# Attention layer with its LayerNorm, router and next-batch input taken from between the batches into the per-head units

## What is computed

```
x = L0_attn_x                                  # (4, 1024, 512) float32
x = x + layernorm(attention(layernorm(x)))     # 4 groups x 4 heads, causal, D = 128
x = x + layernorm(ffn(layernorm(x)))           # top 4 of 32 experts, and a shared expert
# attention: q = rope(x w_aq), k = rope(x w_ak), v = x w_av, softmax(q k + mask) v, times w_ao
# ffn begins with h = rmsnorm(x) * norm_w and logits = h @ router_w.T, of which the top 4 are kept
```

## Time and profile before

| | |
|---|---|
| median of 3 runs | 3898.41 us (3894.68 to 3900.13) |
| profiled execution: its own time | 3902.94 us |
| its span | 3901.0 us |
| PE busy | 3450.9 us, 88% |
| DVE busy | 2377.4 us, 61% |
| ACT busy | 1544.9 us, 40% |
| POOL busy | 1449.2 us, 37% |

### The profile page before, as it was taken

One profiled execution on the slowest core, in us unless ns is written; L12 is line 12 of the kernel. 1 busy time (PEld: TensorE's weight loads), 2 busy tenths in 40 slices (PEclk: granted clock), 3 DMA queues, 4 the chain that ended last, 5 costly groups with the idle time before them and its releaser, 6 DMA issues. The chain is left out here.

```text
span 3901.0 us, 71161 instructions
## 1 busy us (share of the span) xinstructions
PE 3450.9 (88%) x20374; PEld 2950.1 (76%) x20375; DVE 2377.4 (61%) x5034; ACT 1544.9 (40%) x3460; POOL 1449.2 (37%) x1569
## 2 busy tenths in 40 slices
PE   6999996899999699999959999994898999989987
PEld 5888886788888578888858888883687777777766
DVE  5666666666666666666666666667664444444448
ACT  2443443334434243543524344342122444444443
POOL 2333331233333133333303333332422555545548
PEclk9999997899999699999969999995999999999999
DMA  1100002000000200000020000015333676767768
GB/s 54 29 15 15 29 15 100 4 26 17 15 26 17 98 12 18 23 18 18 23 93 15 15 29 15 15 44 203 126 112 95 155 196 159 175 165 171 166 148 277
DMA packets 183202, 287.34 MB, mean 74 GB/s; under 512 B 16544, under 2 KB 69024, under 8 KB 182848
## 3 DMA queue, kind: packets, MB, share of 16 engines
q1 hardware_dynamic: 150432, 204.57, 16.1%
q0 software_dynamic: 32416, 78.43, 10.2%
HBM read 201.93 MB, written 81.02 MB: 73 GB/s over the span
## 5 line engine op out<-in xcount | busy, mean ns | idle before, releaser
L424 DVE TENSOR_TENSOR ptl<-TP,pth 128x512 fp32r<-128x512 f32 (+1 forms) x640 | 407.9, 637 | 281.2 <-ACT pth L560 270.2
L282 POOL TENSOR_SCALAR oTh<-onorm 128x256 fp32r<-128x256 f32 x256 | 104.3, 407 | 1000.3 <-DVE onorm L430 1000.3
L560 ACT CAST pth<-TP 128x512 fp32r<-128x512 f32 (+1 forms) x640 | 349.5, 546 | 300.9 <-PE TP L696 297.1
L613 PE MATMUL O<-pth,vh 128*128 128x256 f32 (+1 forms) x1280 | 399.9, 312 | 22.7 <-DVE ptl L424 22.7
L274 POOL TENSOR_TENSOR work<-work,cst 128x320 f32<-128x320 f32 x128 | 132.9, 1038 | 735.2 <-ACT work L544 735.2
L412 DVE TENSOR_REDUCE negmax<-S 128x1 f32<-128x384 f32 (+7 forms) x512 | 382.3, 749 | 15.9 <-PE S L681 11.1
L613 PE MATMUL S<-wph,xTh 128*128 128x512 f32 (+1 forms) x1024 | 354.6, 346 | 7.0 <-DVE xTl L369 6.7
L615 PE MATMUL O<-pth,vl 128*128 128x256 f32 (+1 forms) x1280 | 359.4, 281 | 0.0
L614 PE MATMUL O<-ptl,vh 128*128 128x256 f32 (+1 forms) x1280 | 358.4, 280 | 0.0
L614 PE MATMUL S<-wpl,xTh 128*128 128x512 f32 (+1 forms) x1024 | 347.2, 339 | 0.0
L615 PE MATMUL S<-wph,xTl 128*128 128x512 f32 (+1 forms) x1024 | 345.7, 338 | 0.0
(11 more groups left out here) (279 smaller groups left out, 9323.1 us busy)
## 6 DMA issues: line engine op xcount, KB each, us to landing
raww<-in_L_ffn_w_dram SPq DMA_DIRECT2D x33, 1024.0 KB, 7.3
prob<-in_L_attn_x_dram SPq DMA_DIRECT2D x9, 2048.0 KB, 9.4
stage<-in_L_attn_w_aq_dram SPq DMA_DIRECT2D x68, 256.0 KB, 2.8
raww<-in_L_ffn_w_dram SPq DMA_DIRECT2D x33, 512.0 KB, 8.2
stage<-in_L_attn_w_ao_dram SPq DMA_DIRECT2D x64, 256.0 KB, 2.6
a<-acc_d SPq DMA_DIRECT2D x64, 256.0 KB, 4.1
acc_d<-x SPq DMA_DIRECT2D x1, 8448.0 KB, 31.5
x_d<-racc SPq DMA_DIRECT2D x4, 2048.0 KB, 14.2
```

The source lines that it names most:

```text
L282: nc.gpsimd.tensor_scalar(slot(oTh, u), onorm[:], 1.0, 1.0, ALU.mult, ALU.mult).then_inc(o_hi, 1)
L424: nc.vector.tensor_tensor(ptl[:, n % 2, 0:w], TP[:, n % 2, 0:w], pth[:, n % 2, 0:w].bitcast(F32), ALU.subtract).then_inc(tp_lo, 1)
L560: nc.scalar.copy(pth[:, n % 2, 0:w], TP[:, n % 2, 0:w]).then_inc(tp_hi, 1)
L613: mm(out, ah, bh, start=first, stop=False)
```

## The change

The work between batches is cut into tiles of 128 tokens and put beside the units. Iteration (b, g) finishes tiles 2g and 2g+1 of batch b-1 and makes tiles 2g and 2g+1 of the x of batch b+1 (modulo 4, so the first batch "finishes" zeros and the last makes an x that is not used). `racc` of a batch is stored to a DRAM tensor `r_d` at its end, and the tiles' transposed x goes to the DRAM tensors `xt_d`, from which `xTh` and `xTl` are reloaded whole, 4 MB, by POOL at unit 12 of the last iteration of a batch. The tiles live in four slots, `slotA` to `slotD`, of the array `work`, and the second half of `S[:, 1]`, called `side`, takes their transposes and logits. Standard deviations come from POOL's `pow` in place of ACT's square root; the logits are plain float32 matmuls, one per 128 rows of h in place of three. The last batch is finished behind the loop, tile after tile.

The tables give the unit at which each step of the two tiles stands: `XN` statistics of x, `XH` its normalisation, `XT_AT` its transpose and split; `RS`, `RN` the same statistics and normalisation of r; `RA` adding x and the statistics of the sum; `RH` its normalisation and product with norm_w; `HT_AT` the transpose of h; `LG_AT` logits and top four.

```diff
+XN, XH = {0: 0, 8: 1}, {1: 0, 9: 1}
+XT_AT = {2: 0, 10: 1}
+RS = {2: 0, 9: 1}
+RA = {3: 0, 11: 1}
+RN = {3: 0, 10: 1}
+RH = {4: 0, 12: 1}
+HT_AT = {6: 0, 14: 1}
+LG_AT = {8: 0, 15: 1}
+EXTRA = {2: 1, 6: 2, 8: 3, 10: 4, 14: 5, 15: 6}
...
+            def scale_shift(done, sem, value, mean, var, sc, ready):
+
+                nc.gpsimd.tensor_scalar(sc[:, 2:3], var, LN_EPS, 1.0, ALU.add, ALU.mult).then_inc(sem, 1)
+                wait_apart(pool, sem, done + value + 1)
+                nc.gpsimd.tensor_tensor(sc[:, 0:1], sc[:, 2:3], half[:], ALU.pow).then_inc(sem, 1)
+                wait_apart(pool, sem, done + value + 2)
+                nc.gpsimd.tensor_scalar(sc[:, 1:2], mean, sc[:, 0:1], -1.0, ALU.mult, ALU.mult).then_inc(ready, 1)
...
+                        if u == RELOAD and reload:
+                            wait_apart(pool, xt_out, it * 64 + 80)
+                            for n, part in enumerate((xTh, xTl)):
+                                nc.gpsimd.dma_start(part[:], xt_d[n]).then_inc(xt_in, 16)
+                        if u in XN:
+                            wait_apart(pool, stx_ready, it * 2 + XN[u] + 1)
+                            scale_shift(pl0, pl, XN[u] * 10, mvx[:, 0:1], mvx[:, 1:2], scx, scx_ready)
...
+                        if u in RA:
+                            wait_apart(pool, str_ready, it * 4 + RA[u] * 2 + 2)
+                            norm_scale(pl0, pl, RA[u] * 10 + 4, mvr[:, 0:1], mvr[:, 1:2], sch, mr, scr_ready)
                         if h == 0:
...
-                            nc.vector.tensor_tensor(racc[:, t], racc[:, t], bank("r", t), ALU.add).then_inc(o_free, 1)
-
-                            wait_apart(v, o_free, b * MB + g * MG + (OUTPUTS.index(("r", t)) + 1 + 2))
-                            nc.vector.bn_stats(stat[:, t], racc[:, t]).then_inc(dve, 1)
...
+                        if u in XT_AT:
+                            k = XT_AT[u]
+                            v.wait_ge(xp_hi, it * SIDE + (EXTRA[u] + 1))
+                            if k:
+                                v.wait_ge(xt_out, it * 64 + (32 + 16))
+                            nc.vector.tensor_tensor(slotC.bitcast(F32R), side, slotB, ALU.subtract).then_inc(xp_lo, 1)
...
+                        if u in RS:
+                            k = RS[u]
+                            v.wait_ge(rd_in, it * 32 + (16 * k + 16))
+                            step(nc.vector.bn_stats(st1[:], slotD), STEPS[("r", k)])
+                            nc.vector.bn_aggr(mvr[:], st1[:]).then_inc(str_ready, 1)
+                        if u in RA:
+                            k = RA[u]
+                            v.wait_ge(rn_done, it * 4 + (2 * k + 1))
+                            v.wait_ge(ra_in, it * 32 + (16 * k + 16))
+                            nc.vector.tensor_tensor(slotD, slotD, slotA, ALU.add).then_inc(x2_ready, 1)
+                            v.wait_ge(x2_ready, it * 2 + (k + 1))
+                            step(nc.vector.bn_stats(st1[:], slotD), STEPS[("a", k)])
+                            nc.vector.bn_aggr(mvr[:], st1[:]).then_inc(str_ready, 1)
...
+                        beside(u)
                         norm_out(u)
                     add_results(PROJECT_LAST)
-                k = k0
-                base2 = v.snap(base + G * GD)
...
+                            nc.scalar.activation(slotD, slotD, ACT.Identity, bias=scr[:, 1:2], scale=scr[:, 0:1]).then_inc(rn_done, 1)
...
+                        beside(u)
                         act.wait_ge(pv_done, it * NPAIR + PAIR_OF[(u, ib)] + 1 + 2)
...
+                        if a == 1 and u - 3 in EXTRA:
+                            if u - 3 in XT_AT:
+                                pe.wait_ge(xp_lo, it * 2 + (XT_AT[u - 3] + 1))
+                            else:
+                                pe.wait_ge(xp_hi, it * SIDE + (EXTRA[u - 3] + 1))
...
+                            for c in range(MC):
+                                ins = nc.tensor.transpose(side[:, c * P:(c + 1) * P], slotA[:, c * P:(c + 1) * P], ident)
+                            ins.then_inc(xp_done, 1)
+                        if u in LG_AT:
+                            pe.wait_ge(xp_hi, it * SIDE + EXTRA[u])
+                            for c in range(MC):
+                                ins = mm(side[:, 0:E], slotB[:, c * P:(c + 1) * P], rwT[:, c], start=c == 0, stop=c == MC - 1)
+                            ins.then_inc(xp_done, 1)
```

More of the change, by code:

```diff
@@ new lines, in _ @@
+            with sp.Fori(0, B - 1) as b:
+                with sp.Fori(0, G) as g:
+                    iteration(b, g)
+                sp.wait_ge(o_free, b * (G * MG) + (G * MG + 2))
+                sp.dma_start(r_d[b].rearrange("(t p) m -> p t m", p=P), racc[:]).then_inc(r_out, 16)
+            with sp.Fori(0, G) as g:
+                iteration(B - 1, g)
+            sp.wait_ge(tp_done, NT + B * G * TG)
+            sp.dma_start(xin, x[B - 1].rearrange("(t p) m -> p t m", p=P)).then_inc(x_in, 16)
@@ L291, in _ @@
                             split_proj(n, it * 10 + 10, it * 80 + 80)
+                    if reload:
+                        landed = pool.to_reg(b * 32 + 32)
+                        pool.wait_ge(xt_in, 32)
+                        pool.wait_ge(xt_in, landed)
+                        pool.sem_inc(xt_ready, 1)
+            with pool.Fori(0, B - 1) as b:
+                with pool.Fori(0, G - 1) as g:
+                    iteration(b, g, False)
+                iteration(b, G - 1, True)
+            with pool.Fori(0, G) as g:
+                iteration(B - 1, g, False)
+            count = 0
+            for k, i in SCALED:
+                t = FINAL[i]
+                pool.wait_ge(str_ready, Z4 + SCALED.index((k, i)) + 1)
+                if k == 0:
+                    scale_shift(ZP, pl, count, mv[:, t, 0:1], mv[:, t, 1:2], fsc[:, t], scr_ready)
+                    count += 2
+                else:
+                    norm_scale(ZP, pl, count, mvh[:, t, 0:1], mvh[:, t, 1:2], fsh[:, t], fmr[:, t], scr_ready)
+                    count += 6
         @block.vector
@@ L327, in link, with stats @@
                 return k + 1
[L329 to L334, removed]
+            def stats(src_of, base, k):
+                for t in range(NT):
+                    nc.vector.bn_stats(stat[:, t], src_of(t)).then_inc(dve, 1)
+                k += NT
                 wait_apart(v, dve, base + k)
@@ L356, in _, with iteration @@
                 center(t, xin[:, t], xin[:, t]).then_inc(xln_ready, 1)
[L358 to L372, removed]
-                    it = v.snap(b * G + g)
-                    gb = v.snap(base + k0 + g * GD)
-                    hi0 = v.snap(hib + NT + g * TG)
+            for t in range(NT):
+                v.wait_ge(tp_hi, t + 1)
+                c4 = xTl[:, :, t * P:(t + 1) * P]
+                nc.vector.tensor_tensor(c4, TP[:, t % 2].rearrange("p (c n) -> p c n", c=MC),
+                                        xTh[:, :, t * P:(t + 1) * P].bitcast(F32), ALU.subtract).then_inc(tp_lo, 1)
+            def iteration(b, g, copies):
+                if True:
+                    it = v.snap(b * G + g)
+                    gb = v.snap(it * GD + first)
+                    hi0 = v.snap(it * TG + NT)
+                    tile = v.snap((b + B - 1) % B * NT + g * 2)
+                    dl0 = it * 12
+                    v.wait_ge(h_out, it * 32 + 16)
                     def lo_tile(t):
@@ L478, in _ @@
[L478 to L498, removed]
@@ new lines, in _ @@
+            act.wait_ge(h_out, 16 + 32 * B * G)
+            act.wait_ge(xt_out, 16 + 64 * B * G)
+            for kind, i in NORMAL:
+                t = FINAL[i]
+                if kind == 0:
+                    act.wait_ge(scr_ready, Z4 + SCALED.index((0, i)) + 1)
+                    nc.scalar.activation(racc[:, t], racc[:, t], ACT.Identity, bias=fsc[:, t, 1:2], scale=fsc[:, t, 0:1]).then_inc(rn_done, 1)
+                elif kind == 1:
+                    act.wait_ge(scr_ready, Z4 + SCALED.index((1, i)) + 1)
+                    nc.scalar.activation(work[:, t], racc[:, t], ACT.Identity, bias=fsh[:, t, 1:2], scale=fsh[:, t, 0:1]).then_inc(rn_done, 1)
+                elif kind == 2:
+                    act.wait_ge(tp_done, ZT + i + 1)
+                    if i >= 2:
+                        act.wait_ge(xp_done, ZX + i - 1)
+                    nc.scalar.copy(stage[:, i % 2], TP[:, i % 2]).then_inc(xp_hi, 1)
+                else:
+                    act.wait_ge(xp_done, ZX + i + 1)
+                    if i >= 2:
+                        act.wait_ge(dl, ZD + LINKS[i - 2])
+                    nc.scalar.copy(lgt[:, i % 2], O[:, i % 2, 0:E]).then_inc(tp_hi, 1)
```

378 lines of the change are left out of this document (252 added, 126 removed).

## The result

The changed kernel takes 3836.7 us (median of 4, 3832.7 to 3845.6) against 3896.6 us of the kernel before beside it (median of 4): a ratio of 0.985, 95% interval 0.983 to 0.987, some 60 us faster. The forecast was 26 us faster, a median of 3872 us. Its direction and the wide range (3795 to 3945 us) hold; the gain is 2.3 times the forecast one, and the time lies outside the forecast's own 3848 to 3896 us.

The account below looks back on a forecast made before the run. PE was taken as nearly full inside iterations and idle between batches. From the profiled 3902.9 us: -228.7 + 12 - 4.3 - 6 + 200 = 3875.9, so a median of 3872 us; range 3795 to 3945 us.

Parts of the forecast that it names:

- What bounds the kernel, and what goes: PE nearly full inside iterations, idle between batches; three gaps go, 228.7 us, plus 4.3 at the start, 6 at the end.
- What is added: Tile work in each of 16 iterations: 12.5 us exposed per iteration, 200 us in all; bounds 8 and 17.5 us.
- Units 9 and 10: Second half of an iteration: statistics, transposes ACT waits for, a copy and an Identity, 1.6 us exposed.
- Units 14 and 15: End of an iteration: the added tile work there was put at 1.5 us exposed.
- The wait for the reload: Between batches: PE waits 4 us each time for xTh and xTl, 12 us in all; bounds 0 and 56 us.
- Unit 2 and unit 3: First half: statistics, sum and ACT's work ahead of onorm delay ptl, stalling PE 1.6 and 2.0 us.
- Unit 12: POOL splits unit 11 behind norm_scale, making ACT 2.8 us late; half covered, so 1.4 us an iteration.
- Rival (a): Inside iterations the chain has more room than single slacks say: 8 us an iteration, 3800 us; chance 0.18.
- Rival (b): POOL's small operations wait 0.4, not 0.1 us, delaying ACT at units 3 and 11: 4 us an iteration, 3936 us; chance 0.16.
- Rival (c): Between batches the reload is late, a second 18.8 us each time: 3928 us; chance 0.12.
- Rival (d): Float32 logits take several passes: 43 us more, 3915 us, or 3894 with unit 15's hidden; chance 0.07.
- Rival (e): Stalls of 2 us lower PE's clock inside iterations, one unit at half pace each: 78 us, 3950 us; chance 0.05.

Follow-up runs that it names:

- dup_r: Changed kernel with the statistics of the sum of results taken twice on DVE, in units 2 and 9; 3856.8 us, an iteration 1.1 us longer.
- behind_rh: Changed kernel with POOL's norm_scale behind the output splits and the step needing it moved from units 4 and 12 to 5 and 13; 3805.8 us.
- reload15: Changed kernel with the reload of xTh and xTl issued in unit 15 of a batch's last iteration, not unit 12; 3846.9 us.
- early: Changed kernel with ACT copying the transposed x out of the side bank before the second exponential in unit 2, not behind it; 3805.2 us.

## Why the prediction was right and wrong

- **What bounds the kernel, and what goes**: right. The gaps were 76 us of which none is left, start and finish came within 1.2 us, and POOL sets the pace of the finish (5.4 to 5.5 us a tile; 5.8 were reckoned). That pace is in part luck: a `pow` takes 0.55 us there and not 0.955, but two of the other operations take 0.56 us and not 0.267, and POOL waits longer between them.
- **The step that failed** is the size of "What is added", 12.5 us an iteration where 11.06 were measured: 23 of the 40 us that the sum is off. The first half had 5.2 us and has 5.5. The second half had 7.3 and has 5.7, and the miss lies in two terms (those of units 11 and 12 were off by 0.4 and 0.5 us, one each way). Units 9 and 10 were put at 1.6 us and cost 0.67: the statistics, the copy and the Identity were counted as exposed, and fitted into waits, so that little more than PE's own transposes shows; dup_r shows that another 0.69 us would not have. Units 14 and 15 were put at 1.5 and cost 0.7: the logits of unit 15 in part fill a stall of PE's own (0.38 us before) that I had not subtracted. Against that the logits themselves are twice as dear as I took them.
- **The wait for the reload**: 12 us forecast, 1.4 measured, another 10.6 of the 40 us (the gaps themselves were 2.2 us longer than reckoned). The cover was right (22 us; 21.6 from issue to projection), the duration was not: I added up two landings that overlap (18.8 us, where both took 15.4). But even 18.8 us fit into the cover. The term that failed is the 4 us allowed at each end for a late POOL: it issued the transfers where the working had it, and PE idles at most 0.5 us ahead of the projection.
- 5.5 us lie in the part that the change does not touch; start, finish and the disturbances make 1.5 us the other way.
- **Why so little mattered so much**: the forecast is the small difference of -239 and +212. The first came out 1% larger, the second, measured 178, 16% smaller. The working named this ("what decides is small against both terms") and its range covered it, but the value in it did not. (By its own terms the work would be even at 14.2 us an iteration, not 14.1.)
- **Unit 2 and unit 3** were named with 1.6 and 2.0 us of stall before `ptl`. Measured are 0.39 and 0.92, with 1.00 us in unit 2 that stands ahead of the scores instead. The sum of units 2 to 4, 4.5 us, came out as 4.7 without PE's own transposes: right in size, and partly for a reason that the working did not have (the side bank).
- **Unit 12**: half of the mechanism is the one named. ACT does wait for POOL's chain; it costs 1.87 us where 1.4 were reckoned, and behind_rh takes all of it away. But the working priced the late split of unit 11, for which ACT waits 0.28 us, and left out that ACT's `Identity` in the same unit needs the chain's result itself, for which it waits 1.92 us. The chain is 3.5 us, not 4.1, since a `pow` takes 0.55 us here.
- **Rival (a)**, more room in the chain: half true, and by places and not everywhere. At five of six places there is none left.
- **Rival (b)**, POOL with waits of 0.4 us: no. They are at most 0.19 us, and ACT waits for `oTl` 0.28 us in unit 12.
- **Rival (c)**, the reload late: no, 6 us to spare.
- **Rival (d)**, several passes for float32: yes, with two records and 0.22 us for each product. The Trainium skill, FP8 and Floating Point Precision, section TensorE Precision Notes, says 4 passes for true FP32; by 0.11 us for each, an estimate, that would be 1.8 us a tile, and the trace has 0.87. Against the 0.45 us of the sum it is 0.4 us a tile more, hidden by the terms that were too high.
- **Rival (e)**, the clock: not in the changed kernel. The granted clock is 1.00 in its units with stalls of 1 us; it does fall, but ahead of the first scores, and in the kernel before as well (below). But the rival was near: in dup_r, where the stall of 0.39 us in unit 2 has grown to 0.98, the clock falls inside the units in seven iterations, for 0.7 to 1.0 us each.

## What to carry over

Slack is a property of a place, not of an engine: read for each place what waits for the engine there, and subtract the waits that PE itself has, or the same added 0.69 us is priced at full where it costs nothing and at nothing where it costs 0.9. Transfers issued together overlapped here, so don't add their landings. Where a forecast is the difference of two large terms, measure the repeated part by marks inside an iteration, which tell 0.1 us where times of executions tell 10, take the mean of several iterations, and look at the granted clock of each before its length is compared. And before work is dropped or moved between units, look whether an engine does it just behind a wait that it could have stood in.

## What was not expected of the hardware

**PE's clock falls for a few us in some iterations of a kernel and not in others.** Behind the same two idle times of PE (1.04 and 1.41 us, ahead of the first scores) the granted clock is 1.00 in one iteration and 0.51 in another, that is at the lower of its two levels. The third iteration of the reload15 kernel, then the same stretch of the changed kernel:

```profile
398.80:405.50 6.70, 6.64 (x27) 5.97 (x28) 4.39 (x10) 3.28 (x10) 0.00 (x0) 0.51 0.28 76
```

```profile
398.80:405.50 6.70, 5.19 (x38) 4.38 (x37) 5.42 (x12) 4.22 (x11) 0.00 (x0) 1.00 0.28 78
```

At this place it costs 0.4 to 1.8 us each time. In the profiled executions it fell on 4 of 16 iterations before, on 6 in the changed kernel, on 10 in reload15 and on none in early. What decides it stays open. Together with a slower DVE instruction it explains part of the scatter between executions: 3.7 to 11.6 us of them in the profiles of three of these kernels. That instruction stands in the thirteenth iteration of the changed kernel and of several variants: one product of the rotation takes 1.50 us on DVE in place of 1.20, at a granted clock of 1.00, and the scores come 0.3 us later.

```profile
1984.57 1.50 DVE L536 TENSOR_TENSOR work<-work,cst 128x640 f32<-128x640 f32 x1
```

**POOL's small operations**: `pow` on 128x1 takes 0.55 us in the attention, where the earlier trace rows has 0.955, and the others 0.19 to 0.33 us (two of them 0.56 us in the finish behind the loop). Why the same operation is slower in the other part of the program was not tried.

```profile
327.15 0.55 POOL L373 TENSOR_TENSOR mr<-sch,half 128x1 f32<-128x1 f32 x1
327.88 0.33 POOL L375 TENSOR_SCALAR sch<-mvr,mr 128x1 f32<-128x1 f32 x1 [0.19 <-POOL mr L373]
```
